# A macaron block on one core: filler products for TensorE, the second FFN's order and its stores changed together

## The reference, cut to what matters

```python
# x: (4, 512, 128), 16 heads of 8, FFN width 512
x = x + 0.5 * ffn(layernorm(x))
x = x + attention(layernorm(x))        # relative positions, softmax, output projection
x = x + 0.5 * ffn(layernorm(x))        # the same weights again

def ffn(x):
    h = layer_norm(x, ln1_g, ln1_b)
    h = gelu(h @ ternary_quant(w1).T + b1)          # (tokens, 512)
    h = layer_norm(h, ln2_g, ln2_b)
    return h @ ternary_quant(w2).T + b2
```

## Time and profile before

| | |
|---|---|
| three runs | 431.8, 432.4, 432.74 us; median 432.4 |
| the profiled execution | 432.4 us, span 430.6 us (first to last instruction) |
| busy | TensorE 351.8 us (82%), VectorE 392.2 (91%), ScalarE 264.1 (61%), GpSimd 176.0 (41%) |
| mean granted clock | 0.970 |

### The profile page before, as it was taken

One profiled execution on the slowest core, in us unless ns is written; L12 is line 12 of the kernel. 1 busy time (PEld: TensorE's weight loads), 2 busy tenths in 40 slices (PEclk: granted clock), 3 DMA queues, 4 the chain that ended last, 5 costly groups with the idle time before them and its releaser, 6 DMA issues.

```text
span 430.6 us, 18108 instructions
## 1 busy us (share of the span) xinstructions
PE 351.8 (82%) x7344; PEld 288.4 (67%) x7344; DVE 392.2 (91%) x565; ACT 264.1 (61%) x642; POOL 176.0 (41%) x216
## 2 busy tenths in 40 slices
PE   1887798785989788897888978889798897984893
PEld 1666675663878677686776867768687686961683
DVE  8879888459999999999999999999999999958695
ACT  1687365336566666666666666666666666633990
POOL 7444756549313415144150431505325053204562
PEclk9999899988899999999999999999999999996899
DMA  7004257574221323213132131322313242010002
GB/s 220 1 2 174 70 144 233 145 203 113 42 70 35 83 45 69 72 34 82 34 73 66 38 81 30 78 64 40 80 22 87 67 76 36 23 52 2 0 26 73
DMA packets 58853, 31.01 MB, mean 72 GB/s; under 512 B 35470, under 2 KB 57454, under 8 KB 58702
## 3 DMA queue, kind: packets, MB, share of 16 engines
q1 hardware_dynamic: 57470, 29.18, 26.5%
q0 software_dynamic: 672, 0.49, 0.8%
q10 hardware_dynamic: 672, 0.80, 0.7%
HBM read 19.44 MB, written 10.88 MB: 70 GB/s over the span
## 4 chain that ended last, share of the span: by engine, by line
DVE 55%; issue 20%; PE 12%; ACT 5%; POOL 3%; SPq 2%; DVEq 1%; DMA 0%; POOLq 0%; ACTq 0%
DVE pT L989 27%; DVE negmax L975 19%; PE pair L1097 2%; DVE xh L796 2%; DVE sqsum L908 1%; PE pair L1055 1%; PE pair L1243 1%; ACT v_rep L679 1%; ACT v_rep L691 1%; DVE x L922 1%; POOL grs L521 1%; PE pair L1199 1%; DVE stat L786 1%; DVE pT L956 1%; PE pair L1284 1%
## 5 line engine op out<-in xcount | busy, mean ns | idle before, releaser
L727 ACT ACTIVATE probs<-pair,negmax 128x512 f32<-128x512 f32 x256 | 173.9, 684 | 104.7 <-DVE negmax L975 104.7
L975 DVE TENSOR_REDUCE negmax<-pair 128x2 f32<-128x1024 f32 x128 | 152.1, 1188 | 6.3 <-PE pair L1216 6.3
L989 DVE STREAM_TRANSPOSE pT<-probs 128x1024 f32<-128x1024 f32 x128 | 157.0, 1227 | 0.4 <-ACT probs L727 0.4
L1199 PE MATMUL pair<-stage_k,stage_c 128*32 128x512 f16 x1024 | 115.5, 399 | 33.0 <-ACT probs L727 30.0
L1205 PE MATMUL pair<-stage_z,stage_q 128*32 128x512 f16 x1024 | 112.5, 387 | 0.0
L584 POOL TENSOR_TENSOR xh<-rowsum,xh 128x16 f32<-128x16 f32 x15 | 43.6, 2904 | 162.8 <-ACT probs L727 162.8
L1216 PE MATMUL pair<-stage_z,stage_q 128*32 128x446 f16 (+59 forms) x1024 | 102.0, 282 | 0.0
L1211 PE MATMUL pair<-stage_z,stage_q 128*32 128x488 f16 (+56 forms) x1024 | 99.5, 278 | 0.0
L1243 PE MATMUL pair<-pT,v_diag 128*32 128x128 f32 (+1 forms) x2176 | 90.5, 267 | 0.0
L1199 PEld LDWEIGHTS pair<-stage_k,stage_c 128*32 128x32 f16 x1024 | 52.6, 140 | 46.3 <-ACT probs L727 36.2
L1243 PEld LDWEIGHTS pair<-pT,v_diag 128*32 128x32 f32 x2176 | 69.3, 111 | 2.1
(11 more groups left out here) (118 smaller groups left out, 366.4 us busy)
## 6 DMA issues: line engine op xcount, KB each, us to landing
stage_z<-z_scratch SPq DMA_DIRECT2D x16, 254.0 KB
stage_q<-qs_scratch SPq DMA_DIRECT2D x116, 24.0 KB
qs_scratch<-pT SPq DMA_DIRECT2D x9, 256.0 KB, 2.6
stage_z<-z_scratch SPq DMA_DIRECT2D x16, 128.0 KB
kc_scratch<-pT SPq DMA_DIRECT2D x8, 256.0 KB
stage_z<-z_scratch SPq DMA_DIRECT2D x16, 127.5 KB
stage_c<-qc_scratch SPq DMA_DIRECT2D x61, 32.0 KB
stage_k<-kc_scratch SPq DMA_DIRECT2D x15, 128.0 KB
```

Of the source, the lines that this page charges most:

```text
L727: nc.scalar.activation(probs[:, q % 6, :], score_pair(q // 2)[:, q % 2, :], ACT.Exp, bias=negmax[:, q % 8:q % 8 + 1], accum_out=rowsum[:, ...
L975: nc.vector.tensor_reduce(negmax[:, 2 * n % 8:2 * n % 8 + 2], score_pair(n)[:, :, :], AX.X, ALU.max, negate=True).then_inc(max_ready, 1)
L989: nc.vector.transpose(pT[:, par, 2 * n:2 * n + 2, :].rearrange("p a s -> p (a s)"), probs[:, 2 * n % 6:2 * n % 6 + 2, :].rearrange("p a s ...
L1199: mm(bank[32 * j:32 * j + 32, :], all_rows[:, 32 * j:32 * j + 32], stage_k[:, par, :], start=True, stop=False, skip_group_check=True)
```

## The change

Three changes are made together.

1. Filler products on TensorE (`fill`), whose results are not read: ten ahead of head 0, 13 behind the last product of the output projection, and eight behind the first group's transposes.
2. The start of the second FFN: VectorE normalises the first two batches ahead of the third's addition and makes the low half of the first group itself (`first_low`); the first hidden product starts when the high half is there; the transposes of the second group move from ahead of the loop into step 0.
3. The second FFN's output: TensorE adds each GELU chunk to the four output tiles of its group when it comes (`out_chunk`: chunks 0 and 1 in step 4, 2 and 3 in step 5, then one a step, two steps behind its GELU), so that the tiles of the groups lie in three pairs of banks in turn. The last group's last square is not summed and split by VectorE: TensorE averages the sum of the first three squares and the last square in fp32 (`last_mean_squares`). Tiles 13 and 15 are stored from ScalarE's queue.

```diff
+OUT_ACT = (NT - 3, NT - 1)
+IDLE_FIRST, IDLE_ADD, IDLE_TURN = 10, 13, 8
...
+        def moments(f, g):
+            return pairs[(1, 2, 3, 1)[g] if f else 1 + g % 2]
+        def chunks(n):
+            return {4: (0, 1), 5: (2, 3)}.get(n, (n - 2,) if HC <= n - 2 < NT else ())
...  SP
             for t in range(NT):
-                sp.wait_ge(ff[1]["x_new"], t + 1)
-                sp.dma_start(ov[t], x[:, t, :]).then_inc(out_done, 16)
+                if t not in OUT_ACT:
+                    sp.wait_ge(ff[1]["x_new"], t + 1)
+                    sp.dma_start(ov[t], x[:, t, :]).then_inc(out_done, 16)
...  POOL, ahead of ffn(1)
             ln_rstd(2, 0)
             ln_rstd(2, 1)
-            ln_low(2, 0)
             ln_rstd(2, 2)
             ln_low(2, 1)
...  ScalarE, behind ffn(1)
+            for t in OUT_ACT:
+                act.wait_ge(ff[1]["x_new"], t + 1)
+                act.dma_start(ov[t], x[:, t, :]).then_inc(out_done_act, 16)
...  VectorE, ffn
-                    if 0 <= m < NT and c:
+                    if 0 <= m < NT - f and c:
...
-                    if 0 <= m < NT and c == HC - 1:
+                    if 0 <= m < NT - f and c == HC - 1:
...  VectorE, ahead of ffn(1)
-            for b in range(B):
+            for b in range(2):
                 add_attention(b)
                 ln_stats(2, b)
-                if b:
-                    ln_xhats(2, b - 1)
-            ln_xhats(2, B - 1)
+            ln_xhats(2, 0)
+            ln_xhats(2, 1)
+            dve.wait_ge(ln[2]["xT"], 2)
+            nc.vector.tensor_tensor(xT_low[:, 0:S], xT[:, 0:S], xT_high[:, 0:S], ALU.subtract).then_inc(first_low, 1)
+            for b in range(2, B):
+                add_attention(b)
+                ln_stats(2, b)
+            for b in range(2, B):
+                ln_xhats(2, b)
...  TensorE
+            def last_mean_squares(s):
+                pe.wait_ge(s["sq_summed"], sums(NT - 2))
+                pe.wait_ge(s["squared"], NT)
+                for part in (sqsum[:, :], sq[:, (NT - 1) % 3, :]):
+                    for t in range(4):
+                        ins = mm(moments(1, B - 1)[:, 0, SQ0 + t:SQ0 + t + 1], part[:, t * 128:(t + 1) * 128],
+                                 w2c[:, 0, D:D + 1], start=False, stop=True, skip_group_check=True)
+                ins.then_inc(s["sq_mean"], 1)
+            def out_chunk(s, m):
+                g, c = divmod(m, HC)
+                if m == 0:
+                    pe.wait_ge(x_attn, B)
+                if m == 2 * HC:
+                    pe.wait_ge(ln[2]["xT"], 2 * B)
+                if m == 3 * HC:
+                    pe.wait_ge(s["x_new"], 4)
+                pe.wait_ge(s["gelu"], m + 1)
+                for t in range(4):
+                    ins = mm(out_tile(1, 4 * g + t), ge[:, m % 8, t * 128:(t + 1) * 128], w2c[:, c, :],
+                             start=c == 0 and t % 2 == 0, stop=c == HC - 1, skip_group_check=True)
+                    if c == HC - 1:
+                        ins.then_inc(s["ffn"], 1)
...  TensorE, ffn
-                        pe.wait_ge(ln[2 * f]["xT_low"], g + 1)
+                        if f == 1 and n == 0:
+                            pe.wait_ge(ln[2]["xT"], 1)
+                        elif f == 0 or g:
+                            pe.wait_ge(ln[2 * f]["xT_low"], g + 1 - f)
...
                         mm(ps[n % 2], w1T[:, k], xT_high[:, tokens], start=True, stop=False)
+                        if f == 1 and n == 0:
+                            pe.wait_ge(first_low, 1)
                         mm(ps[n % 2], w1T[:, k], xT_low[:, tokens], start=False, stop=True).then_inc(s["hid"], 1)
+                    if f == 1:
+                        for m in chunks(n):
+                            out_chunk(s, m)
                     t = n - 5
-                    if 0 <= t < NT:
+                    if 0 <= t < NT and f == 0:
...
+                    if f == 1 and n == NT + 1:
+                        last_mean_squares(s)
...
+            def fill(bank, count):
+                for _ in range(count):
+                    mm(ps[bank], w1T[:, 0:128], w1T[:, :], start=True, stop=True)
...
+            fill(6, IDLE_FIRST)
             pe.wait_ge(staged_pool, 16 * LOADS_POOL)
             head(0, 0, 16 * LOADS_EVEN, True)
...
                 direct(H - 1, b).then_inc(wo_mm, 1)
+            fill(1, IDLE_ADD)
             for t in range(4):
                 ln_turn(2, t)
-            for t in range(4):
-                ln_turn(2, 4 + t)
+            fill(1, IDLE_TURN)
             ffn(1)
```

More of the change, by code:

```diff
@@ L192, in macaron_kernel @@
               for f in range(2)]
+        first_low = sem("first_low")
         pos_mm = sem("pos_mm")
@@ L242, in macaron_kernel @@
         out_done = sem("out_done")
+        out_done_act = sem("out_done_act")
         def x_made(eng, f, t):
@@ L765, in _ @@
             ffn(1)
+            ov = out.rearrange("b (t p) d -> (b t) p d", p=128)
+            for t in OUT_ACT:
+                act.wait_ge(ff[1]["x_new"], t + 1)
+                act.dma_start(ov[t], x[:, t, :]).then_inc(out_done_act, 16)
         @block.vector
@@ L889, in ffn @@
                         dve.wait_ge(s["sq_mean"], g + 1)
-                        mean = moments(g)[:, :, 0:2 * (D + 1)].rearrange("p a (t n) -> p a t n", t=2)[:, :, :, D]
+                        mean = moments(f, g)[:, :, 0:2 * (D + 1)].rearrange("p a (t n) -> p a t n", t=2)[:, :, :, D]
                         nc.vector.tensor_scalar(gmean[:, cols4].rearrange("p (a t) -> p a t", a=2), mean,
@@ L1056, in ln_turn, with mean_squares @@
                                     ident[:, :]).then_inc(s["turned"], 1)
-            def mean_squares(s, g):
+            def last_mean_squares(s):
[20 more added lines that the diff above has]
+                        ins.then_inc(s["ffn"], 1)
+            def mean_squares(f, g):
+                s = ff[f]
                 pe.wait_ge(s["sq_split"], 2 * g + 2)
@@ L1078, in ffn @@
                         mm(ps[n % 2], w1T[:, k], xT_high[:, tokens], start=True, stop=False)
+                        if f == 1 and n == 0:
+                            pe.wait_ge(first_low, 1)
                         mm(ps[n % 2], w1T[:, k], xT_low[:, tokens], start=False, stop=True).then_inc(s["hid"], 1)
+                    if f == 1:
+                        for m in chunks(n):
+                            out_chunk(s, m)
                     t = n - 5
-                    if 0 <= t < NT:
+                    if 0 <= t < NT and f == 0:
                         g = t // 4
-                        if t == 0 and f == 0:
+                        if t == 0:
                             pe.wait_ge(w2_ready, 1)
                             pe.wait_ge(const_ready, 1)
-                        if t == 4 and f == 0:
+                        if t == 4:
                             pe.wait_ge(pos_f, 1)
-                        if t == 0 and f == 1:
-                            pe.wait_ge(x_attn, B)
                         if t % 4 == 0:
@@ L1096, in ffn @@
                         for c in range(HC):
-                            ins = mm(out_tile(t), ge[:, (4 * g + c) % 8, k], w2c[:, c, :],
+                            ins = mm(out_tile(f, t), ge[:, (4 * g + c) % 8, k], w2c[:, c, :],
                                      start=(c == 0), stop=(c == HC - 1))
                         ins.then_inc(s["ffn"], 1)
-                    if n % 4 == 0 and n >= 8 and n < 4 * B + 8:
-                        mean_squares(s, (n - 8) // 4)
+                    if n % 4 == 0 and 8 <= n < 4 * B + 8 - 4 * f:
+                        mean_squares(f, (n - 8) // 4)
+                    if f == 1 and n == NT + 1:
+                        last_mean_squares(s)
                     if n == 1 and f == 0:
                         turn_weights(1, ps[3])
-                    if n in TURN_STEPS[f] and (f == 0 or n):
+                    if n in TURN_STEPS[f]:
                         for t in range(4):
```

15 lines of the change are left out of this document (7 added, 8 removed).

## The result

The changed kernel took 430.0 us (median of 20 runs, 428.45 to 432.19) against 432.4 us for the kernel before on the same chip (20 runs): a ratio of 0.9945, interval [0.9933, 0.9958]. The profiled execution took 429.9 us, with a mean granted clock of 0.974. So it is faster, inside the predicted range, by 2.4 us instead of the forecast 3.8.

What follows compares the result with a forecast made beforehand. VectorE's row maxima and transposes through attention were the last-ending chain, then ScalarE set the FFN's pace. Terms: -1.5 - 0.3 - 2.05 + 1.05 - 0.5 - 0.5 = -3.8 us, from 432.4 to 428.6 us; range 427.2 to 430.9.

Steps and rivals of the forecast that it cites:

- First fill, -1.5 and -0.3: Ten products keep TensorE's clock up: head 0's first transpose 1.5 us sooner, head 1's slow start 0.3 us less.
- the rival that it gains nothing: Head 0: the clock falls all the same or transfers hold it, giving 430.4 us; chance 0.12.
- a few tenths: Start of head 0: if the ten products start late, they push the scores by a few tenths of a us at most.
- First GELU, -2.05: Start of the second FFN: the first GELU starts at 393.7 us in place of 395.75.
- TensorE gives back +1.05: First GELU to last evacuation: late third-group tokens, then hidden products, five chunks and transposes on TensorE, cost 1.05 us.
- the first rival: Second FFN's light steps: the clock falls onto the chunk steps and costs some 1.7 us, giving 430.3 us; chance 0.22.
- its sign of failure: Granted clock after the fills: a clock of 0.50 behind either fill would show the prediction wrong.
- the predicted 11.45: First GELU to the last batch's evacuation: 10.4 us before the change, with TensorE's +1.05 us on top.
- the bad bound: First GELU to evacuation: +1.6 us in place of +1.05 if POOL holds up VectorE's first square sum as well.
- Chunks and unsplit squares, nothing: Second FFN's end: TensorE's savings, up to 2.7 us, count nothing, covered by VectorE's queue; the squares' 1.8 us cost nothing.
- POOL collision, -0.5: Tail: without VectorE's sum beside it, POOL's scaling of the third group is faster, and its update comes 0.5 us sooner.
- Two queues, -0.5: Last stores: with two of the last four on ScalarE's queue, issues no longer stand in a row, 0.5 us less.

Runs made afterwards that it cites:

- the changed kernel again: The changed kernel itself measured once more, with no edit: median 429.28 us, ratio 0.9955 to the kernel before.
- the light fills: The changed kernel with 2, 6 and 3 more unread products in steps 1, 2 and 3 of the second FFN: median 428.12 us, ratio 0.9930 to before.
- the one-queue kernel: The changed kernel with all stores on SP's queue: median 429.35 us, ratio 0.9944 to the kernel before.
- the tile kernel: The changed kernel with the second FFN's output tile by tile and all squares split, as before: median 429.23 us, ratio 0.9947 to before.

## Why the prediction was right, and the term that was off

*First fill, -1.5 and -0.3.* Right in cause and size: -1.36 at head 0 and another -0.53 by the attention's end, -1.89 together; the rival that it gains nothing is excluded by the kernel without it. That the second part came near its -0.3 is in part luck: with the clock of head 1 coming and going, the two together are -1.67 to -2.26 in the twelve profiles with this fill. What I had allowed as "a few tenths" for late products did not come in: the 0.43 us at the first scores lie ahead of the change, since the transfer was issued 0.38 us later, and in another profile (the changed kernel again) the scores waited 1.01 us for their transfer behind the same fill.

*First GELU, -2.05.* Measured -2.04. Of that 1.68 is the new order as a whole (no POOL subtraction, no second turn on the path) and 0.36 the fills, by the kernel without them; the prediction had not divided it.

*"TensorE gives back +1.05".* This is the step that failed: it measured +2.05. Its sum took the clock as kept, and the first rival, the fall in the light steps, happened. It came where the prediction had not put its sign of failure: not right behind a fill, but 5 us later. The chunks at 398.09 us ran at the lower level, and the fall cost 0.9 us, shown by the light fills that take it away, and by the one-queue kernel, which without the fall has the same 11.53 us. In other profiles it cost 1.3 to 1.4 us. The rival's price of 1.7 us was too high: the last transposes ended 12.39 us behind the first GELU, against 11.24 with the light fills, so TensorE came 1.15 us later, and ScalarE, late by VectorE's sum, hid 0.29 us of that. The rule of the Trainium skill weighed there ("TensorE: Matmul & The Clock Gate", "Part 4: PE-mode transpose") spoke for this rival. The 0.50 at 396 us agrees with it, though no run separates transposes from an idle TensorE; the one-queue kernel, with 1.00 through the same light steps, shows that it does not decide each execution.

At the full clock the piece took 11.53 us, near the predicted 11.45, but for another reason, so the nearness is luck. I had TensorE's queue of chunks as the limit and VectorE's sum only as the bad bound. TensorE's queue was sized well (its last transposes were done at 11.24 us), but the runs show VectorE's sum as the latest and the turn behind a chunk as second. The hold-up itself was under-sized: normalising beside POOL's two 128x512 operations took 2.95 us, where I had allowed 1.1 + 0.6 for one. The trace of the kernel before held a row that shows more for one such operation, in the normalising beside POOL's subtraction of the earlier trace rows:

```profile
392.33 2.01 DVE L796 TENSOR_SCALAR xh<-x,mv,rs 128x128 f32<-128x128 f32 x4
```

*Chunks and unsplit squares, nothing; POOL collision, -0.5.* Both right: -0.54 in the piece, 0.51 by the tile kernel, and TensorE's end ahead of the mean, though by 0.96 us and not by 2 to 3. I had priced the eight one-column fp32 products of the last squares (sixteen records in the trace) at 1.8 us at most; from 419.92 to 421.84 they took 1.9. VectorE's order was the cover, and lifting it gave 0.84 us.

*Two queues, -0.5.* Right.

## What to carry to other kernels

A filler does not hold the clock for what stands behind it, so ask what comes next: if light steps still follow, the fall can move to them, and it is cheap where the engine waits anyway (0.36 us here) and dear where it sets the pace (0.9 to 1.4 us). When several engines feed one step, price each one's arrival and expect the second-latest to take over when the latest is mended. A sum of pieces between fixed events of the trace settles terms of half a microsecond that the medians of whole runs, with 1 us of scatter upstream, cannot.

## What the runs showed of the hardware

The same instructions, in separate executions, kept the clock at 1.00 or lost it to 0.50, at head 1 in two profiles of one kernel and on the steps of the chunks in two that differ only in the queues of two stores: the state of the clock does not follow from the instructions alone.

VectorE's four normalisings took 1.08 us alone, 1.70 beside one 128x512 operation of POOL and a power (395.22 us) and 2.95 beside two, while POOL's 128x512 subtraction kept its 1.16 us (1.15 in the earlier trace rows). The first row below (VectorE's line L809 in the changed kernel, 397.5 to 400.5 us; durations in ns: min, median, max) shows how: two of the four took 1.28 and 1.24 us, each from the start of one POOL operation to just behind its end, and the other two 0.33 us. It can go the other way: in the kernel before, the same subtraction of POOL took 1.67 us (second row), 0.02 us behind the start of VectorE's square sum at 402.49 us. That the one that starts later bears the collision is my reading of these rows; no run tests it.

```profile
L809 DVE TENSOR_SCALAR xh<-x,mv,rs x4: 334/785/1282, 397.6 to 400.2; 128x128 f32<-128x128 f32 x4
```

```profile
402.51 1.67 POOL L496 TENSOR_TENSOR v_rep<-xT,v_rep 128x512 f16<-128x512 f32 x1 [0.80 <-ACT xT L651]
```

Four fp32 products with one column (eight records) take 1.02 us together, as much as a chunk's four with 129 columns (1.95 us for two chunks).
